# Graph attention in a fused four-layer kernel: the weighted sum in two halves, the inverses' spread and the features in slots of their own, the masked minimum one slot later with a ring of seven

## What is computed

```python
def gat_layer(x, adj, W, a_self, a_neigh, b):
    feat = jnp.einsum('nf,hfo->hno', x, W)
    attn_self = jnp.einsum('hno,ho->hn', feat, a_self)
    attn_neigh = jnp.einsum('hno,ho->hn', feat, a_neigh)
    e = attn_self[:, :, None] + attn_neigh[:, None, :]
    e = jax.nn.leaky_relu(e, LRELU_ALPHA)
    e = e + MASK_VAL * (1.0 - adj)[None, :, :]
    alpha = jax.nn.softmax(e, axis=-1)
    out = jnp.einsum('hnm,hmo->hno', alpha, feat) + b[:, None, :]
    out = jnp.transpose(out, (1, 0, 2)).reshape(out.shape[1], -1)
    return jax.nn.elu(out)
```

## Time and profile before

| | |
|---|---|
| median of 3 runs | 1146.29 us (1140.42 to 1147.44) |
| the profiled execution | 1144.96 us, of which its span is 1143.1 us |
| the GAT within the span | about 12 to 191 us |
| TensorE clock over the span | 0.938 of full |
| PE, DVE, ACT, POOL busy over the span | 91%, 74%, 53%, 36% |

### The profile page before, as it was taken

The page is one execution under the profiler, slowest core; times in us unless marked ns, Lnnn a source line. Parts: engine busy times, 40 slices in busy tenths (PEclk is TensorE's granted clock), DMA queues, the critical chain, the costliest instruction groups (busy, mean ns, idle before and its releaser), DMA issues.

```text
span 1143.1 us, 20323 instructions
## 1 busy us (share of the span) xinstructions
PE 1040.5 (91%) x6046; PEld 847.9 (74%) x6046; DVE 851.0 (74%) x2622; ACT 604.9 (53%) x1685; POOL 411.9 (36%) x350
## 2 busy tenths in 40 slices
PE   5899995499999458999999999999998999999997
PEld 3555663346666247899999999999987888888886
DVE  6878876427775478977777777777777888888887
ACT  4678774143333238777777777777863222222221
POOL 5778873350000433332333333221322232323321
PEclk9869987569999769999999999999999999999999
DMA  8900002111111221101011010000010111111111
GB/s 253 373 12 1 2 1 68 42 51 44 44 47 46 69 97 38 48 1 38 6 42 38 1 34 1 2 1 1 2 43 14 43 41 55 41 55 41 45 52 37
DMA packets 55459, 53.46 MB, mean 47 GB/s; under 512 B 5536, under 2 KB 48864, under 8 KB 55376
## 3 DMA queue, kind: packets, MB, share of 16 engines
q1 hardware_dynamic: 52560, 46.87, 13.1%
q0 software_dynamic: 1536, 4.20, 1.2%
q10 hardware_dynamic: 1280, 1.38, 0.5%
HBM read 43.25 MB, written 9.18 MB: 46 GB/s over the span
## 4 chain that ended last, share of the span: by engine, by line
PE 76%; DVE 8%; ACT 5%; POOL 5%; issue 4%; DMA 1%; another core or an unknown queue 0%; ACTq 0%; DVEq 0%; POOLq 0%
PE bank L57 13%; PE bank L58 13%; PE bank L59 13%; PE bank L907 7%; PE bank L928 5%; PE bank L804 4%; PE bank L812 4%; PE bank L829 4%; PE bank L917 3%; PE bank L929 2%; POOL rest L1344 2%; PE bank L631 2%; PE bank L615 1%; ACT alpha L1015 1%; PE bank L886 1%
## 5 line engine op out<-in xcount | busy, mean ns | idle before, releaser
L1414 POOL TENSOR_TENSOR rot_s<-swap,rq 128x512 f32<-128x512 f32 x64 | 88.5, 1383 | 198.3 <-ACT swap L1194 198.3
L1070 ACT ACTIVATE silu<-bank 128x512 f32<-128x512 f32 x66 | 39.5, 599 | 175.1 <-PE bank L59 175.1
L1955 DVE TENSOR_TENSOR o_ring<-bank,o_ring 128x256 fp32r<-128x256 f32 x128 | 54.3, 424 | 83.7 <-ACT o_ring L1223 82.9
L1207 ACT ACTIVATE prob<-prob,pmin 128x128 f32<-128x128 f32 (+1 forms) x256 | 113.2, 446 | 2.9 <-DVE pmin L1936 2.8
L907 PE MATMUL bank<-kv,norm 128*128 128x128 f32 (+1 forms) x512 | 106.1, 330 | 6.4 <-DVE norm L1929 6.0
L1759 DVE SCALAR_TENSOR_TENSOR xs<-bank,wt,xs 128x256 f32<-128x256 f32 x264 | 109.0, 476 | 0.2
L1362 POOL TENSOR_TENSOR gate_r<-gate_w,gate_r 128x256 fp32r<-128x256 f32 x31 | 36.5, 1176 | 177.2 <-ACT gate_r L1063 177.2
L1223 ACT ACTIVATE o_ring<-bank 128x256 fp32r<-128x256 f32 x128 | 48.4, 378 | 80.1 <-PE bank L929 79.9
L57 PE MATMUL bank<-wo_r,o_ring 128*128 128x256 f32 x256 | 84.1, 328 | 0.0
L1936 DVE CUSTOM_DVE_ANT_0 prob<-bank,causal 128x128 f32<-128x128 f32 (+1 forms) x256 | 80.2, 350 | 0.1
L1737 DVE TENSOR_TENSOR hidf<-silu,bank 128x512 f32<-128x512 f32 x66 | 45.4, 688 | 46.3 <-ACT silu L1070 44.6
(11 more groups left out here) (293 smaller groups left out, 3121.8 us busy)
## 6 DMA issues: line engine op xcount, KB each, us to landing
gate_w<-in_Wg SPq DMA_DIRECT2D x33, 128.0 KB, 2.1
up_w<-in_Wu SPq DMA_DIRECT2D x33, 128.0 KB, 2.2
down_w<-in_Wd SPq DMA_DIRECT2D x33, 128.0 KB, 2.3
w_all<-in_w_gate SPq DMA_DIRECT2D x8, 512.0 KB, 10.3
w_all<-in_w_up SPq DMA_DIRECT2D x8, 512.0 KB, 10.3
w_all<-in_w_down SPq DMA_DIRECT2D x8, 512.0 KB, 10.4
wq_g<-in_Wq SPq DMA_DIRECT2D x4, 1024.0 KB, 5.5
wo_g<-in_Wo SPq DMA_DIRECT2D x4, 1024.0 KB, 5.6
```

What stands on the lines that cost most here:

```text
L1207: ins = act.activation(prob[:, u % 4, nt * P:nt * P + (nt + 1) * P], prob[:, u % 4, nt * P:nt * P + (nt + 1) * P], ACT.Exp, bias=pmin[:, u ...
L1414: pool.tensor_tensor(rot_s[:, m % 2].rearrange("p (b n) -> p b n", b=2), swap[:, m % 2].rearrange("p (b n) -> p b n", b=2), bcast(tab[:, 1 ...
```

## The change

The pipeline is re-timed, and no instruction is added or removed on any engine but waits and semaphore increments. In numbers of slots:

- the masked minimum of DVE moves from slot k+2 to k+3, and what follows a unit (exponent, transpose, copy) one slot with it. The ring `alpha` has 7 buffers and not 6. `copied_by_dve` takes the even units, so that DVE's copy still stands in a slot without a `leak`.
- `weigh` is cut in three: line 636 (now 626, `spread_inverses`) comes first, in slot 4j+9, and frees `row_sum` by a semaphore of its own, `inv_spread`; the eight matmuls of line 631 (now 640) come as four in slot 4j+10 and four in slot 4j+11.
- `divide`, `exp_out` and `positive` move from slot 4j+10 to 4j+12, `elu` from 4j+11 to 4j+13.
- `prep` goes from slot 8r-4 to 8r-5, `features` from 8r-3 and 8r-2 to 8r-4 and 8r, `copy_features` from 8r-1 to 8r+1. `turn_x1` and `add_x1` move by one slot.
- `rest` stands elsewhere in SBUF, and there is one slot more at the end.

```diff
-RING = 6
+RING = 7
...
-        LAST = ALL + 11
+        LAST = ALL + 12
...
-            j, off = divmod(k - lag - 9, QUAD)
+            j, off = divmod(k - lag - 10, QUAD)
...
-            return k % 2 == 1 and k % 16 != 15
+            return k % 2 == 0 and k % 16 != 14
...
-                def weigh(j):
-
-                    r, c = divmod(j, QUADS)
-                    for h4 in range(QUAD):
-                        pe.wait_ge(*alphaT_copied(QUAD * j + h4))
-                    if c == 0:
-                        pe.wait_ge(S["feat_copied"], r + 1)
+                def spread_inverses(j):
+
                     if j >= 2:
                         pe.wait_ge(S["g_norm"], j - 1)
-                    for mc in range(NT):
-                        for h4 in range(QUAD):
-                            h = QUAD * c + h4
-                            pe.matmul(OB[j % 2][h4 * GO:(h4 + 1) * GO, 0:N], feat[r % 2][:, mc, h * GO:(h + 1) * GO],
-                                      alphaT[:, j % 2, h4, mc, :], start=mc == 0, stop=mc == NT - 1)
                     pe.wait_ge(S["row_inv"], j + 1)
...
-                    mm.then_inc(S["av_done"], 1)
+                    mm.then_inc(S["inv_spread"], 1)
+
+                def weigh(j, mc):
+
+                    r, c = divmod(j, QUADS)
+                    if mc == 0:
+                        for h4 in range(QUAD):
+                            pe.wait_ge(*alphaT_copied(QUAD * j + h4))
+                        if c == 0:
+                            pe.wait_ge(S["feat_copied"], r + 1)
+                    for h4 in range(QUAD):
+                        h = QUAD * c + h4
+                        mm = pe.matmul(OB[j % 2][h4 * GO:(h4 + 1) * GO, 0:N], feat[r % 2][:, mc, h * GO:(h + 1) * GO],
+                                       alphaT[:, j % 2, h4, mc, :], start=mc == 0, stop=mc == NT - 1)
+                    if mc == NT - 1:
+                        mm.then_inc(S["av_done"], 1)
...
-                    if (r := starts_in(k, 4)) is not None:
+                    if (r := starts_in(k, 5)) is not None:
                         prep(r)
-                    if 0 <= k - 4 < ALL:
-                        turn(k - 4)
+                    if 0 <= k - 5 < ALL:
+                        turn(k - 5)
                     if 0 <= k + 1 < ALL:
                         edges(k + 1)
                     for nt in range(NT):
-                        if (r := starts_in(k, 3 - nt)) is not None:
+                        if (r := starts_in(k, 4 - 4 * nt)) is not None:
                             features(r, nt)
-                    if (j := quad_at(k, 0)) is not None:
-                        weigh(j)
-                    if (r := round_at(k, 17)) is not None:
+                    if (j := quad_at(k, -1)) is not None:
+                        spread_inverses(j)
+                    for mc in range(NT):
+                        if (j := quad_at(k, mc)) is not None:
+                            weigh(j, mc)
+                    if (r := round_at(k, 18)) is not None:
                         turn_x1(r)
...
-                        act.wait_ge(S["av_done"], j - 1)
+                        act.wait_ge(S["inv_spread"], j - 1)
...
-                    if 0 <= k - 3 < ALL:
-                        exps(k - 3)
...
+                    if 0 <= k - 4 < ALL:
+                        exps(k - 4)
...
-                if (j := quad_at(k, 1)) is not None:
+                if (j := quad_at(k, 2)) is not None:
                     positive(j)
...
+                    dve.wait_ge(S["inv_spread"], j + 1)
                     dve.wait_ge(S["av_done"], j + 1)
...
-                    if 0 <= k - 2 < ALL:
-                        edges(k - 2)
+                    if 0 <= k - 3 < ALL:
+                        edges(k - 3)
```

More of the change, by code:

```diff
@@ L176, in build @@
         alpha = sb_early("alpha", [P, RING, 2 * N])
-        rest = sb_early("rest", [P, 2 * N])
         ctx_all = sb_early("ctx_all", [FC, B * N])
@@ L182, in build @@
         first_use.close()
+        rest = sb_early("rest", [P, 2 * N])
         alphaT = sb_early("alphaT", [P, 2, QUAD, NT, N])
@@ L1041, in graph_attention @@
                         copy_z(k)
-                    if 0 <= k - 3 < ALL:
-                        exps(k - 3)
-                    if 0 <= k - 5 < ALL and not copied_by_dve(k - 5):
-                        copy_T(k - 5)
-                    if (j := quad_at(k, 1)) is not None:
+                    if 0 <= k - 4 < ALL:
+                        exps(k - 4)
+                    if 0 <= k - 6 < ALL and not copied_by_dve(k - 6):
+                        copy_T(k - 6)
+                    if (j := quad_at(k, 2)) is not None:
                         exp_out(j)
-                    if (r := starts_in(k, 1)) is not None:
+                    if (r := starts_in(k, -1)) is not None:
                         copy_features(r)
```

14 lines of the change are left out of this document (7 added, 7 removed).

## The result

The changed kernel took 1158.7 us, median of 7 runs (1147.87 to 1168.39), beside 1146.29 for the kernel before: a ratio of 1.0096, 95% interval [1.0067, 1.0125]. So it is slower by about 1%, where a small gain was forecast. The graph attention ends with the last `add_x1` at 196.1 us, against 190.7 before.

The account below looks back on a forecast made before the run. PE was taken to bound the stage at the low clock, POOL at the high. Terms 7.3 - 4.0 + 2.6 - 9.0 + 0.5 = -2.6 us against 1144.96 gave 1142.4, stated as 1143, range 1127 to 1170.

Parts of the forecast that it names:

- the quad of layer 0 that was to find the high level: Quads 0 to 4: all four low is +7.3 us; one was assumed to run at the high clock, -4.0.
- the eight quads at 8.8 us: Layer 1 behind the clock's rise: eight quads that took 79.4 us take 70.4 at the high clock, -9.0.
- quad 4 to 5: Start of layer 1: the clock rises after half a low quad, 11.8 us instead of 9.12, +2.6.
- depth: front and end: The deeper pipeline's extra slot at front and back costs between 0 and 2.3 us; 0.5 was taken.
- Check (3): Granted clock stays low from 42 to 87 us but for a stretch or two, then 1.00 from about 100 to 185.
- POOL's own instructions are the floor: High-clock quads: without POOL's 0.38 us wait for DVE's division, the 9.01 us quad would be 8.63.
- check (2): High-level quads take 8.6 to 8.9 us; above 9.0 another engine or ACT's wait for the division bounds.
- Check (1): DVE's wait for POOL's half of the leaky ReLU is near nothing, its wait for the PE block under 5 us.
- gains no more than its own wait for DVE, 0.38 us a quad: Late minimum at the high clock: POOL gains between 0 and 0.38 us a quad; 0.2 was taken.
- Check (4): Behind the stage, the distance from the last `add_x1` to the span's end stays as before, within 3 us.
- Layer 0 low and layer 1 high: The forecast's own clock case, by itself spanning 1136 to 1152 us; chance 0.38.
- alternates as now: Rival: PE's small waits for ACT keep the clock swinging, only the POOL term is left, 1140 to 1145; chance 0.08.

Follow-up runs that it names:

- a1_whole: The changed kernel with the weighted sum and the inverses back in one block, in slot 4j+10: 1147.42 us, ratio 1.001.
- h1_prep_apart: The changed kernel with PE's `prep` in slot 8r-7 and DVE's in slot 8r-6, away from the division: 1155.12 us, ratio 1.009.
- i2_add_behind: The changed kernel with `prep` in slots 8r-7 and 8r-6 and `add_x1` of rounds 4 to 6 behind the division: 1152.68 us, ratio 1.005.
- c1_min_early: The changed kernel with DVE's masked minimum back in slot k+2, nothing else moved: 1159.97 us, ratio 1.010.
- b1_kick: The changed kernel with two extra matmuls, results unused, in each of slots 5 to 9: 1153.65 us, ratio 1.004.
- d1_fill: The changed kernel with one extra matmul, result unused, in each PE slot from 9 to 28: 1147.66 us, ratio 1.002.
- f1_prep_back: The changed kernel with `prep` of PE and DVE back in slot 8r-4: 1154.96 us, ratio 1.010.
- i3_whole_add: The changed kernel with sum and inverses in one block, `prep` in slots 8r-7 and 8r-6, `add_x1` behind the division: 1131.9 us, ratio 0.989.

## Why the prediction was wrong, point by point

The measured 1158.7 us lies within the stated range of 1127 to 1170, but a gain of 3 us was forecast and the change lost 12. Two terms of the sum failed: the quad of layer 0 that was to find the high level, and the eight quads at 8.8 us. The parts of the stage, in us against the kernel before (first profile of the changed kernel, and the second one):

| part | forecast | first | second |
|---|---|---|---|
| quads 0 to 4 | +7.3 - 4.0 = +3.3 | +7.9 | +8.8 |
| quad 4 to 5 | +2.6 | -0.3 | +1.7 |
| quads 5 to 13 | -9.0 | -3.2 | +1.4 |
| depth: front and end | +0.5 | +1.0 | +1.5 |
| sum | -2.6 | +5.4 | +13.4 |

**The clock: right in mechanism, one term too kind.** A quad of layer 0 at the low level was put at 13.0 us and took 13.2. That the cut block loses the clock in layer 0 is shown by `a1_whole`: the block whole gives 1.001, against 1.0096, with intervals that do not meet. The step that failed is "I take it that one of them finds the high level, -4.0": in neither of the two profiles of the changed kernel did one, and quads 0 to 4 took 7.9 and 8.8 us more than before where +3.3 was forecast. It had no row behind it; the same text said that no rise had come without a whole block, and the forecast should have followed that. That a whole block was not always enough stood in the earlier trace rows, unused: the one at 71.11 us raised nothing until 86.65. Check (3) held up to 130 us.

**The quads at the high level: the step that failed.** The text put all eight at 8.8 us, from "POOL's own instructions are the floor". Every second quad is 8.79 us, but the others are 9.9 to 10.6, so check (2) failed, and the eight took 3.2 us less than before in the first profile and 1.4 more in the second, where 9.0 less was forecast. Two things were missed. DVE, with 20.81 of 23.90 us at the high level nearly as full as POOL, became the bound, and what the change did to *its* order was looked at only about the division: `prep` moved to the slot ahead of it, and `add_x1` from behind it to ahead. It was written that "nothing is added" when these moved, and no price was given. By `h1_prep_apart`, `i2_add_behind` and the rows above, the two cost 1.6 to 1.7 us in each of quads 8, 10 and 12, most of it not as their own time but because they shift DVE's minimum against POOL's two-input instruction. With both repaired the forecast's 8.8 is there: 8.36 to 8.91. The signs that the prediction named for being wrong were waits of ACT or PE; in the long quads DVE waited for neither, and the time went into the duration of its own instructions.

**The late minimum: the wait went and came back as duration.** Check (1) held, no wait for line 1355 remains, and DVE waits only 3.5 us for PE's halves in the low stretch (4.5 in the first 420 us). But the minimum's mean rose from 484 to 606 ns. The step by which POOL "gains no more than its own wait for DVE, 0.38 us a quad", of which half was taken, took the wait away without asking what the instruction collides with when it starts earlier. `c1_min_early`, at 1.010 as the changed kernel, shows that in this order it brought nothing measurable.

**Depth.** `positive` of quad 0 comes 4.2 us later, since it stands two slots later, and the end is 3.2 us shorter: +1.0, where 0.5 was taken from 0 to 2.3.

**Fall in layer 1.** The clock can fall in layer 1 too: in the first profile for 3.4 us at 130.9, without a longer quad to show for it, in the second for 17.1 us, which makes one quad 14.73 instead of 10.6. `b1_kick`, `c1_min_early`, `d1_fill` and `f1_prep_back` each show a stretch of that length as well. `h1_prep_apart` and `i2_add_behind` held it for 61.4 and 71.7 us on end. What decides it from one execution to the next is not settled.

**Behind the stage.** Check (4) held in both profiles: the rest of the span is 2.4 us shorter, within the 3 us named.

**The rivals.** Layer 0 low and layer 1 high was the right case; in both profiles the loss, 5.4 and 13.4 us, came out of the likeliest case's own terms, in the second with one low stretch of layer 1 besides. The execution at the median was not profiled. For "alternates as now" spoke the rule of the Trainium skill, "TensorE: Matmul & The Clock Gate", section "A second HAM failure mode: psum-queue depth-cycling", that micro-idles between groups of matmuls make the clock swing. In `i3_whole_add` PE was idle for 6.90 of 81.90 us with the clock high all the time, so such idles alone did not bring a fall here.

**Open.** `i3_whole_add` differs from the kernel before in the late minimum with its ring of seven, in the slots of `features` and `copy_features`, in which units DVE copies, and in the slot of PE's `prep`; the block is whole in both, and DVE's `prep` and `add_x1` stand to the division as before. Which of these makes 1.1%, and how much of it is the clock, was not taken apart. It has 4 runs.

## What to carry to other kernels

Before a block of PE work is cut for smoothness, look at which blocks the clock's rises follow in the trace; if only the dense block does, keep it whole, or the stage runs at half speed with a full PE. When a wait of DVE for POOL is removed, look at what both engines do at the moment at which the instruction then starts, and put an instruction that reads PSUM there. And for each instruction that a re-timing moves, ask on which side of the one that others wait for (here the division) it lands, and which instructions behind it are pushed into another engine's way.

## What the runs showed of the hardware

- More work made the kernel faster: one matmul of 64 rows by 256 columns in 20 slots took the changed kernel from 1.0096 to 1.002, and in the thin slots of the kernel before, up to slot 63, it gave 0.994.
- A busy PE did not mean a high clock: 40.34 of 41.00 us busy, low all the time (`b1_kick`).
- DVE's minimum, which reads two tensors in SBUF, takes 1.42 to 1.49 us instead of 0.41 when it starts soon after POOL's two-input instruction; DVE's instructions that read a bank ran beside it at 0.40 and 0.42. The Trainium skill, "SBUF — State Buffer", section "Who interferes with whom", says that a DVE instruction with two SBUF inputs contends with a GpSimd instruction that reads SBUF, and calls the shared port an exclusive lock. The rows agree for POOL's line 1355 and not wholly for its line 1352, which also reads SBUF: a minimum at 148.85 took 0.41 us in the middle of it (148.04 to 149.97), while one that started with it (151.54 beside 151.49) took 0.83.
- The clock's record has nothing ahead of the first change: 84.81 us at the low level read 1.00.
